# A mixture-of-experts kernel: the expert stage's TensorE program written out tile by tile

## The reference

```python
x = x + 0.5 * ffn(layernorm(x))
x = x + attention(layernorm(x))          # 16 heads of 16
x = x + 0.5 * ffn(layernorm(x))

def ffn(x):                              # E = 32 experts, the top 4 of each token
    scores = softmax(x @ Wg)
    weights, indices = top_k(scores, 4)
    y = 0
    for e in range(32):                  # at most C = 2048 tokens each
        tok, w = tokens and weights of expert e
        xg = x[tok]
        out = (silu(xg @ W1[e]) * (xg @ W3[e])) @ W2[e] * w[:, None]
        y = y.at[tok].add(out)
    return y + (silu(x @ Ws1) * (x @ Ws3)) @ Ws2
```

## Time and profile before

| what | us |
|---|---|
| time, median of 3 runs | 3115.54 (3107.31 to 3118.48) |
| span of the profiled execution, first to last instruction | 3024.1 |
| what lies outside the span, against the median | 91.4 |
| expert stage of layer 0, first turn to last turn | 128.6 to 401.0 |
| expert stage of layer 1, first turn to last turn | 2566.9 to 2840.2 |
| TensorE busy, whole span | 2726.5 (90%) |

### The profile page before, as it was taken

The page is one execution under the profiler, slowest core; times in us unless marked ns, Lnnn a source line. Parts: engine busy times, 40 slices in busy tenths (PEclk is TensorE's granted clock), DMA queues, the critical chain, the costliest instruction groups (busy, mean ns, idle before and its releaser), DMA issues. The chain is left out here.

```text
span 3024.1 us, 60105 instructions
## 1 busy us (share of the span) xinstructions
PE 2726.5 (90%) x16843; PEld 1083.2 (36%) x16844; DVE 2052.2 (68%) x3845; ACT 2319.4 (77%) x3563; POOL 712.5 (24%) x1002
## 2 busy tenths in 40 slices
PE   5799989969999989999999999999999975999972
PEld 5488845512222212222212222211112162888541
DVE  6744458747786777786876886877868867444354
ACT  4644435569999999999999999999999945444320
POOL 1555568620000000000000000000000014555576
PEclk9999999989999999999999999999999985999986
DMA  5555555520010010010010010010001026455644
GB/s 180 151 155 156 152 124 138 138 52 3 5 25 3 5 25 3 5 24 3 5 25 3 5 25 4 4 24 4 3 3 32 3 86 186 151 155 156 115 124 124
DMA packets 132050, 195.29 MB, mean 65 GB/s; under 512 B 22365, under 2 KB 99325, under 8 KB 130429
## 3 DMA queue, kind: packets, MB, share of 16 engines
q1 hardware_dynamic: 104188, 117.00, 13.8%
q0 software_dynamic: 27648, 75.53, 10.3%
HBM read 124.85 MB, written 67.50 MB: 64 GB/s over the span
## 5 line engine op out<-in xcount | busy, mean ns | idle before, releaser
L1683 ACT ACTIVATE RB<-psS 128x1024 f32<-128x1024 f32 x1920 | 1766.1, 1200 | 8.8 <-PE psS L1601 8.6
L1635 PE MATMUL psO<-RB,values 128*32 128x512 f32 x7680 | 1026.1, 606 | 0.5 <-ACT RB L1683 0.5
L1601 PE MATMUL psS<-WE 51*128 51x512 f16 x3840 | 695.3, 387 | 80.6 <-DMA WE<-shift_d 11.2
L1601 PEld LDWEIGHTS psS<-WE 51*128 51x128 f16 x3840 | 174.3, 93 | 1093.9 <-ACT RB L1683 1071.5
L661 POOL DMA_INDIRECT xg<-xn_d,index x320 | 305.0, 953 | 223.0 <-issue 136.5
L685 PE MATMUL psH<-WE,xgt 128*128 x1280 | 341.7, 390 | 0.0
L1547 POOL COPY values<-WE 128x512 f32 x12 | 7.0, 611 | 1319.5 <-PE psO L1635 1319.5
L749 ACT ACTIVATE gate<-psH 128x128 f32<-128x128 f32 x320 | 88.9, 278 | 249.2 <-PE psH L685 249.2
L734 DVE TENSOR_TENSOR hid<-gate,psH 128x128 f32<-128x128 f32 x320 | 92.1, 288 | 261.0 <-ACT gate L749 261.0
L1635 PEld LDWEIGHTS psO<-RB,values 128*32 128x32 f32 x7680 | 151.3, 108 | 277.3 <-issue 245.2
L1699 DVE TENSOR_SCALAR part<-psO 128x512 f32<-128x512 f32 x256 | 171.8, 671 | 114.8 <-PE psO L1601 114.8
(11 more groups left out here) (250 smaller groups left out, 3121.7 us busy)
## 6 DMA issues: line engine op xcount, KB each, us to landing
pair_d<-ob SPq DMA_DIRECT2D x320, 128.0 KB, 1.8
WE<-part_d SPq DMA_DIRECT2D x84, 128.0 KB
xn_d<-ws SPq DMA_DIRECT2D x64, 128.0 KB, 1.7
WE<-in_W SPq DMA_DIRECT2D x2, 4096.0 KB, 23.6
part_d<-raw SPq DMA_DIRECT2D x32, 256.0 KB, 3.0
xg<-xn_d,index POOLq DMA_INDIRECT x320
RA<-in_x SPq DMA_DIRECT2D x8, 512.0 KB, 8.9
head_d<-sums SPq DMA_DIRECT2D x128, 32.0 KB, 1.6
```

The lines of the kernel that those rows point to most:

```text
L1601: return pe.matmul(ps, K[r][rows, kt * P:(kt + 1) * P], Q[r][rows, at:at + BLK], start=True, stop=True)
L1635: last = pe.matmul(psO[g % 2][32 * j:32 * (j + 1), :], values[:, r, j % 2, kt, :], weights, start=(kt == 0), stop=(kt == KT - 1))
L1683: act.activation(probs[n % RING][:, half * 2 * BLK:(half + 1) * 2 * BLK], psS[m % HELD][:, :], ACT.Exp, scale=SCALE).then_inc(sem("exped"), 1)
```

## The change

TensorE's program in `experts` is written out for all 160 tiles instead of running in a hardware loop. Every wait gets a constant. The expert numbers come from one register load for four tiles, into two banks of four registers, done at the end of step j = 0, 4, 8 and so on for the four tiles after the current four. Three waits are dropped, since a wait of the same or an earlier step implies each: `xgt_ready` before the turn, `hid_ready` before the multiply upwards, and `hidt_ready` before the turn of the hidden rows. The other engines' programs stay as they are.

```diff
-                def step(j, s, lap):
-                    if has(j, 2, NJ):
-                        pe.wait_ge(gathered[(s + 2) % U], lap(2) * 16 + (16 + L * 16 * NJ // U))
-                        if has(j, 0, NJ):
-                            pe.wait_ge(sem("xgt_ready"), j + 1)
...
-                    if has(j, 1, NJ):
-                        e = pe.snap(owner[(s + 1) % U], min_val=0, max_val=E - 1)
-                        pe.wait_ge(sem("xgt_ready"), j + 2)
-                        if has(j, -1, NJ):
-                            pe.wait_ge(sem("hid_ready"), j)
...
-                    if has(j, 2, NJ):
-                        pe.reg_load(owner[(s + 2) % U], tile_expert[0:1, bass.ds(j + 2, 1)])
-                    if has(j, 0, NJ):
-                        pe.wait_ge(sem("hid_ready"), j + 1)
-                        if has(j, -2, NJ):
-                            pe.wait_ge(sem("hidt_ready"), j - 1)
...
-                skewed(pe, NJ, U, step)
+                owner = [[pe.alloc_register(f"owner{n}_{u}_{L}") for u in range(U)] for n in range(2)]
+
+                def fetch(group):
+                    pe.reg_load(owner[group % 2], tile_expert[0:1, group * U:(group + 1) * U])
...
+                def turn(j):
+                    pe.wait_ge(gathered[j % U], 16 * (1 + j // U) + L * 16 * NJ // U)
...
+                def up(j):
+                    expert[j] = e = pe.snap(owner[j // U % 2][j % U], min_val=0, max_val=E - 1)
+                    pe.wait_ge(sem("xgt_ready"), j + 1)
...
+                def turn_hidden(j):
+                    pe.wait_ge(sem("hid_ready"), j + 1)
...
+                def down(j):
+                    e = expert.pop(j)
+                    pe.wait_ge(sem("hidt_ready"), j + 1)
+                    if j >= 2:
+                        pe.wait_ge(sem("ob_ready"), j - 1)
...
+                fetch(0)
+                for j in range(-2, NJ + 1):
+                    if j + 2 < NJ:
+                        turn(j + 2)
+                    if 0 <= j + 1 < NJ:
+                        up(j + 1)
+                    if 0 <= j < NJ:
+                        turn_hidden(j)
+                    if 0 <= j - 1 < NJ:
+                        down(j - 1)
+                    if j >= 0 and j % U == 0 and j + U < NJ:
+                        fetch(j // U + 1)
```

More of the change, by code:

```diff
@@ L668, in _ @@
                 pe.sem_inc(sem("x_turned"), U)
-                owner = [pe.alloc_register(f"owner{u}_{L}") for u in range(U)]
-                def step(j, s, lap):
-                    if has(j, 2, NJ):
-                        pe.wait_ge(gathered[(s + 2) % U], lap(2) * 16 + (16 + L * 16 * NJ // U))
-                        if has(j, 0, NJ):
-                            pe.wait_ge(sem("xgt_ready"), j + 1)
-                        for c in range(DC):
-                            last = pe.transpose(psX[s % 2][:, c * P:(c + 1) * P], xg[:, (s + 2) % U, c * P:(c + 1) * P], ident[:, :])
-                        last.then_inc(sem("x_turned"), 1)
-                    if has(j, 1, NJ):
-                        e = pe.snap(owner[(s + 1) % U], min_val=0, max_val=E - 1)
-                        pe.wait_ge(sem("xgt_ready"), j + 2)
-                        if has(j, -1, NJ):
-                            pe.wait_ge(sem("hid_ready"), j)
[L684 to L687, removed]
-                    if has(j, 2, NJ):
-                        pe.reg_load(owner[(s + 2) % U], tile_expert[0:1, bass.ds(j + 2, 1)])
-                    if has(j, 0, NJ):
-                        pe.wait_ge(sem("hid_ready"), j + 1)
-                        if has(j, -2, NJ):
-                            pe.wait_ge(sem("hidt_ready"), j - 1)
[L694 to L701, removed]
@@ L703, in _ @@
-                skewed(pe, NJ, U, step)
+                owner = [[pe.alloc_register(f"owner{n}_{u}_{L}") for u in range(U)] for n in range(2)]
+                def fetch(group):
+                    pe.reg_load(owner[group % 2], tile_expert[0:1, group * U:(group + 1) * U])
+                expert = {}
+                def turn(j):
+                    pe.wait_ge(gathered[j % U], 16 * (1 + j // U) + L * 16 * NJ // U)
+                    for c in range(DC):
+                        last = pe.transpose(psX[j % 2][:, c * P:(c + 1) * P], xg[:, j % U, c * P:(c + 1) * P], ident[:, :])
+                    last.then_inc(sem("x_turned"), 1)
@@ new lines, in up @@
+                def up(j):
+                    expert[j] = e = pe.snap(owner[j // U % 2][j % U], min_val=0, max_val=E - 1)
+                    pe.wait_ge(sem("xgt_ready"), j + 1)
+                    for c in range(DC):
+                        last = pe.matmul(psH[j % 2][:, :], xgt[:, j % 2, c * P:(c + 1) * P],
+                                         WE[:, e, c * 2 * H:(c + 1) * 2 * H], start=(c == 0), stop=(c == DC - 1))
+                    last.then_inc(sem("up"), 1)
+                def turn_hidden(j):
+                    pe.wait_ge(sem("hid_ready"), j + 1)
+                    pe.transpose(psG[j % 2][:, :], hid[:, j % 2, :], ident[:, :]).then_inc(sem("h_turned"), 1)
@@ new lines, in down @@
+                def down(j):
[3 more added lines that the diff above has]
+                        pe.wait_ge(sem("ob_ready"), j - 1)
+                    pe.matmul(psO[j % 2][:, :], hidt[:, j % 2, :], WE[:, e, DC * 2 * H:],
+                              start=True, stop=True).then_inc(sem("down"), 1)
+                fetch(0)
[10 more added lines that the diff above has]
+                        fetch(j // U + 1)
```

## The result

| | before | after |
|---|---|---|
| time, median of 5 launches, us | 3108.2 (3105.8 to 3118.5) | 3092.5 (3083.4 to 3096.5) |
| ratio after to before | | 0.9939, 95% interval 0.9918 to 0.9959 |
| in two later sets of launches | 3115.6 and 3118.9 | 0.9947 (0.9930 to 0.9964) and 0.9955 (0.9939 to 0.9970) |
| span of the profiled execution | 3024.1 | 3093.4 |

The kernel became faster by 15.7 us in the medians, 16.8 and 14.2 in the later sets. The prediction had 16.5.

The account below looks back on a forecast made before the run. TensorE sets the expert stages' pace, its sequencer too slow to cover the loop's branch. Gain 17.5 us, less 0.5 for late gathers and 0.5 for last tiles, is 16.5: from 3115.5 to 3099.0 us, range 3092 to 3112.

Parts of the forecast that it names:

- the forecast: Both expert stages: all the loop's excess goes and the load is covered; 16.5 us gained, 3099.0 us; chance 0.62.
- B: Rival at TensorE's register load: four numbers cost four loads, 1.23 us, taking 13 us of the gain; 3112 us; chance 0.15.
- C: Rival in the expert loop: the excess belongs to DVE, ACT or POOL closing their loops; no change, 3115 us; chance 0.10.
- The loop's excess: TensorE's expert loop, both layers: time above undisturbed steps of 1.6275 us, 17.5 us (16.7 to 18.1), all to be gained.
- the late gathers: POOL's gathers in the expert stages: one late gather per layer shows more with less cover; cost 0.25 us a layer, 0.5 in all.
- the sequencer's time over a round: TensorE's expert loop: three steps of 1.55 us and one of 2.1 make 6.75, against 6.5 of matmuls for four tiles.
- The cover of the load: After the wait for hidt, before the next turn: some 1.05 us left for the four-number load, so it costs nothing.
- its signs: Changed trace, expert stages: every step from tile 4 to the late tiles 1.63 us, 147 in 239 to 240, 139 in 226 to 227.
- The last tiles: End of each expert stage: DMA engines set the pace, nothing gained, shorter cover bites sooner; cost 0.25 us a layer, 0.5 in all.
- 91.4 us above the span: Whole kernel: the median of the runs lies 91.4 us above the profiled span of 3024.1, and the change touches nothing there.
- Rival A: Written-out expert stages: instruction fetch is not hidden, 2.16 us for each of 30 packets, costing 65 us; 3164 us; chance 0.07.
- The evidence from attention: Attention, 660 to 1090 us: 26 packets in 430 us, the same rate, without TensorE waits by issue; so fetch costs nothing.

Follow-up runs that it names:

- the loop kernel without waits: Kernel before with its hardware loop and per-tile loads, only the three waits dropped: 175.8 us for the 108 steps; launches 3115.2 us, ratio 0.9984 to before.
- fulfilled waits: Loop kernel without the three waits, with a wait for the long-landed weights' loads in the place of each: 186.5 us for the 108 steps, 187.6 in layer 0.
- eight steps: Kernel before with eight steps in TensorE's loop instead of four, the wait value adapted: 178.1 us for the 108 steps, 178.7 in layer 0.
- after again: The changed kernel, unchanged, launched and profiled again: ratio 0.9947 (0.9930 to 0.9964) to before.
- paced gathers: After, with POOL waiting before each gather for the one before last to land, except the first two of each sixteen: 200.6 and 202.1 us for the 108 steps.
- eight buffers: After, with eight gather buffers and semaphores for xg instead of four: ratio 0.9987 (0.9975 to 0.9999) to before.

## Why the prediction was right in size and wrong in its chances

**The number.** 16.5 us predicted, 15.7 in the medians, 16.0 in the two stages' traces. The mechanism, a sequencer too slow for its branch over a round, is shown by the experiments on branch, waits and loads. That the median of 3092.5 is within 3092 to 3112 is luck: it is 6.5 us below the 3099.0 named, because the launches of before now have a median 7.4 us lower than the 3115.5 that I started from.

**The chances.** They failed. The likeliest class I named was a change within 0.5%, 0.48; the measured ratio is 0.61% below 1, and its whole interval lies below 1. The step is in "How the numbers follow": from a sum of 0.53% I put 0.24 of the forecast, B's 0.15 and C's 0.10 on the side of no change, so that the classes contradicted the sum. The premise was that the kernel can be measured to about 0.5%, 15.6 us; the interval came out at 0.2% to either side, some 6 us, which leaves 15.7 us in no doubt. B and C had little to stand on. C was excluded by rows that I cited myself (consumers 0.8 to 1.1 us early, idle by issue), and 0.10 was too much for it. B needed each number to cost a load; one row would have decided it, and there was none, but the load took 332 ns.

**The loop's excess, 17.5 us.** On the chip without late increments (see the last section) the loop kernel without waits, which reaches the same pace, gives it most cleanly: from tile 4 to 151 in layer 0 it takes 239.6 us, from 4 to 143 in layer 1 226.5, against 249.0 and 233.9. That is 9.4 and 7.4, 16.8 us, 17.0 by my sum after the late gathers' 0.5.

**Why it was lost.** The working added up the sequencer's time over a round, 6.75 against 6.51 us, and this was right. Where that time is the longer one, the sequencer's trace has no gap of more than 0.15 us and the round is as long as the sequencer's: 6.73 to 6.76 us before, 6.86 to 6.90 with fulfilled waits, 13.2 for eight steps. Where it is the shorter one, in the loop without waits, in after and in the program written out with the old waits and loads, the gaps are there and the step is TensorE's 1.628. In the round before, the turn behind the branch is only 0.04 us late; the rest is lost in the step that follows. The weight loads of that turn, and of the product one step on:

```profile
305.16 0.20 PEld L677 LDWEIGHTS psX<-ident,xg 128*128 128x128 f32 x2 [0.27 <-issue]
...
306.57 0.30 PEld L700 LDWEIGHTS psO<-WE,hidt 128*128 128x128 f32 x2 [0.19 <-issue]
```

**The cover of the load.** 1.05 us predicted from ACT's `hidt`, 0.9 measured. Nothing hung on the difference.

**The late gathers.** Sized at 0.25 us a layer from a single trace in which the steps 112 to 128 took 27.5 and 27.1 us. In after's profile they take 29.5 and 29.2, 3.3 us over 16 steps of 1.6277, and so tiles 4 to 151 of layer 0 took 243.0 us and 4 to 143 of layer 1 229.4, not the 239 to 240 and 226 to 227 that the prediction named as its signs. That would have taken 4 us off the gain, had not the kernel before lost as much where it was profiled again (30.2 and 30.7, some 1 us of that the loop's; after on that chip 29.5 and 30.1). The term was wrong in size for either kernel and right for their difference.

**The last tiles.** Predicted at a cost of 0.25 us a layer; within the scatter (28.6 and 30.8 before, 29.5 and 31.3 after, 28.6 and 30.8 in after again), nothing to see. That their pace isn't TensorE's was right; what sets it was the one row that empty slots gather.

**Span and launch.** "91.4 us above the span" was a wrong reading: span and launch differ by some 2 us, and the profile must have come from another chip than the launches. The difference of the two kernels did not need it.

**Rival A.** TensorE's fetch queue brings 150 packets instead of 123, 13 of them in the first stretch of 242 us, and the steps around them are 1.63 us. Straight code is not held up there, with DMA engines 54% busy. The evidence from attention was weaker than I wrote: from 660 to 1090 the matmuls have no idle by issue, but the weight loads have 248, 68.0 us in all and 0.4 us the longest.

## What to carry to other kernels

When an engine's loop costs a little each round, look in its trace for gaps between its sequencer's instructions. If there are none, the sequencer sets the pace, and its time over a round is what counts, with the mean of its loads and not the median. Deleting waits that others imply can then free the loop at no cost in code; a longer loop only helps if its sum leaves some margin. Time a small edit in the stages that it doesn't touch, too: attention lost 10 us, two thirds of what the edit had won, probably because its jumps had moved. And let padding slots read different rows.

## What the runs showed of the hardware that I had not expected

- A register load of four numbers takes 332 ns, of one 308. The Trainium skill (Runtime: NRT & Kernel Launch, Instruction fetch mechanics) has about 200 ns for each register even in bulk; here it is 8 ns for each further one.
- At the gather of tile 113, in both layers and in every kernel but the one with paced gathers (2.0 us), POOL stands still for 3.2 to 3.8 us. On two of the chips something follows: in after's profile DVE and ACT take up work 1.5 to 2.4 us after TensorE finished it. The copy of 315.37 is for the turn that ended at 312.99.

```profile
315.37 0.42 DVE L739 COPY xgt<-psX 128x256 f32<-128x256 f32 x1 [2.40 <-PE psX L679]
```

```profile
314.02 0.38 ACT L768 ACTIVATE ob<-psO 128x256 f32<-128x256 f32 x1 [1.19 <-PE psO L699]
315.43 0.28 ACT L759 ACTIVATE gate<-psH 128x128 f32<-128x128 f32 x1 [1.02 <-remote]
```

  It comes behind runs of gathers 1.26 us apart, more with eight buffers, and not on the third chip. Its cause is open.
- 128 reads of one DRAM row by a gather hold the DMA engines busy at 0.98 for 133 GB/s; with distinct rows it is 0.51 for 164.
- The same kernel takes 3022 us on one chip (one launch) and 3107 to 3126 on two others; by the profiles nearly all of it lies in the stages that combine.
